# Loading the second weight blocks of summed products through ScalarE's DMA queue instead of SyncE's

## The chip, the cores and the metric

The kernel runs on one core of a Trainium2 chip. The metric is the device time of one execution in microseconds (us); lower is better.

## The reference

Two layers of a residual network, each a full 2048 x 2048 linear layer with bias and a low-rank adapter of rank 16 that is chosen by batch element:

```python
x = x + (x @ W0.T + b0 + (x @ A0[ids0].T) @ B0[ids0].T)
x = x + (x @ W1.T + b1 + 2 * (x @ A1[ids1]) @ B1[ids1])
```

x has 8 batch elements of 512 tokens and 2048 features, all in fp32; ids0 and ids1 name one of 32 adapters for each batch element.

## The kernel before

Since nothing nonlinear stands between the layers, the kernel first makes one matrix of both (V in `v_t`, then the combined matrix in `wc_t`), and then multiplies x by it. A preamble of some 178 us turns layer 0's weights with TensorE and prepares the adapters. Then comes one main loop of six passes. Passes 0 and 1 (`pl < PRE`) multiply the two layers' matrices and read their left operand from `v_t`; passes 2 to 5 multiply the combined matrix `wc_t` with two batch elements each.

Each pass is a 2 x 2 block product by Strassen's scheme: seven products, in the order M5, M3, M2, M4, M1, M7, M6, each of 1024 x 1024 by 1024 x 1024. A product has 16 steps, and a step s is half of a row of tiles: 4 weight tiles of 128 x 128, each multiplied three times against 512 columns (high part times high part, low times high, high times low, L1248 to L1250), which keeps fp32 accuracy. So a step is 12 matmuls. Four of the products (M5, M3, M2, M4) have adapter matmuls between their first steps (L1179, L1182, L1183), and in the later passes M3, M4, M7 and M6 have short ones at their ends (L1193).

In five of the seven products (M5, M2, M1, M7, M6) the weight operand is a sum or a difference of two blocks of the matrix. For a step of these, two blocks of 256 KB come from memory: the **first** into one of four buffers `w_raw` (`RAW`), the **second** into one of three buffers `w_second` (`RAW2`). From there:

- GpSimd (POOL) adds the second to the first in place (L710), once both semaphores, `wa_loaded` and `wb_loaded`, say that the blocks have landed, and counts up `w_summed`.
- ScalarE (ACT) rounds the sum to its high part `w_hi` (L752, `w_split_hi`), in a ring of three, so it also waits for the step three before (`step_done`).
- VectorE (DVE) subtracts it from the sum for the low part `w_lo` (L862), and TensorE (PE) starts the step when `w_lo_ready` says so.

In M3 and M4 the weight operand is one block, and POOL has nothing to do.

All transfers are issued by SyncE (SP), in one order written out in the program. In turn g of its loop SP calls `load_w(g + 6)`. That waits until `w_lo` of the step four before is made, issues the first block (L468), waits until the sum of the step three before is made, and issues the second block (L474). Behind that in the same turn stand loads of the x operand for this or the next pass (L480, L483, most of them in M7 and M6 and in M3), adapter blocks (L514), and stores of finished output tiles (L556, L559), each with its own waits. ACT makes the high part of step g + 2 in its turn g, then high parts of x (L765) and of the adapter (L780).

At the end of the preamble SP issues eight x loads, the adapter blocks, and the loads of steps 0 to 3; the second block of step 3 needs the first sum. Only behind it stand two stores of V (L443), sixteen x loads (L480), a store of 2 MB (`ag_t`, L635), which waits for VectorE, and the loads of step 4.

```python
                if s >= RAW:
                    sp.wait_ge(w_lo_ready, s - RAW + 1)
                (oh, dh), *second = PRODUCTS[i][1]
```

Of the kernel before, what the change touches and what calls it, by code (L numbers as in the profile page):

```python
# [4 lines left out]
P = 128  # L5
# [12 lines left out]
PRODUCTS = (  # L18
# [7 lines left out]
)  # L26
NPROD = len(PRODUCTS)
M5, M3, M2, M4, M1, M7, M6 = range(NPROD)
# [18 lines left out]
def two_layer_lora_kernel(nc, x_t, ids0, ids1, w0_t, w1_t, bias0, bias1,  # L47
# [6 lines left out]
    BATCH, KT, _, T = x_t.shape  # L54
    MT = w0_t.shape[0]
    DIM = KT * P
    SLOTS, RANK, _ = lora_b0.shape
    MH = MT // 2
    KH = KT // 2
    KS = KH // 2  # L60
    SW = KS * P
# [3 lines left out]
    STEPS = MH * 2  # L65
    RAW = 4
    RAW2 = 3
# [6 lines left out]
    PRE = MT * P // (2 * T)  # L74
    NPL = PRE + BATCH // 2
    NQ = NPL * NPROD
    NG = NQ * STEPS
# [3 lines left out]
    ORDER = [(2 * mp + mm, h) for mp in range(MH // 2) for h in range(2) for mm in range(2)]  # L81
# [59 lines left out]
    def x_tiles_at(g, at):  # L141

        out = []
        for k in range(KH):
            q, j = divmod(g - at[k], STEPS)
            if j == 0 and 0 <= q < NQ - 1:
                out.append((q + 1, k))
        return sorted(out)
# [9 lines left out]
    def is_sum_w(g):  # L158
        return len(PRODUCTS[(g // STEPS) % NPROD][1]) == 2

    SUM_STEPS = [0]
# [5 lines left out]
    NU = len(UNITS)  # L167
# [14 lines left out]
    with ctx:  # L182
# [236 lines left out]
        def w_source(pl):  # L419
            return v_t if pl < PRE else wc_t  # L420
# [10 lines left out]
        def _(sp):  # L431
# [17 lines left out]
            def load_w(s):  # L449
                q, j = divmod(s, STEPS)  # L450
                pl, i = divmod(q, NPROD)
                m, h = ORDER[j]
                r = s % RAW
                w_t = w_source(pl)
                if s == 0:
                    for i_v in range(2):
                        sp.wait_ge(v_stored[i_v], 8 * 16 // 2)
                if s == M2 * STEPS:
                    for i_v in range(2):
                        sp.wait_ge(v_stored[i_v], NU * 16 // 2)  # L460
                if pl == PRE and j == 0 and i in (M5, M2):
                    for b in range(4):
                        sp.wait_ge(out_stored[b], (PRE if i == M2 else 1) * MH * 16)
                if s >= RAW:
                    sp.wait_ge(w_lo_ready, s - RAW + 1)
                (oh, dh), *second = PRODUCTS[i][1]
                col = (dh * KH + h * KS) * P
                sp.dma_start(w_raw[:, r, :], w_t[oh * MH + m, :, col:col + SW]).then_inc(wa_loaded[r], 16)  # L468
                for oh, dh in second:
                    n = SUM_STEPS[s]  # L470
                    if n >= RAW2:
                        sp.wait_ge(w_summed, n - RAW2 + 1)
                    col = (dh * KH + h * KS) * P
                    sp.dma_start(w_second[:, n % RAW2, :], w_t[oh * MH + m, :, col:col + SW]  # L474
                                 ).then_inc(wb_loaded[n % RAW2], 16)

            def load_x(pl, half, th, k):
                b = block_no(half, th)
# [159 lines left out]
            for g in range(NG):  # L638
                q, j = divmod(g, STEPS)
                pl, i = divmod(q, NPROD)  # L640
                s = g + 6
# [72 lines left out]
        def _(act_e):  # L714
# [29 lines left out]
            def w_split_hi(s):  # L744
                r = s % RAW
                if is_sum_w(s):
                    act_e.wait_ge(w_summed, SUM_STEPS[s + 1])
                else:
                    act_e.wait_ge(wa_loaded[r], (s // RAW + 1) * 16)
                if s >= RING:  # L750
                    act_e.wait_ge(step_done, s - RING + 1)
                nc.scalar.activation(flat(w_hi[:, s % RING, :, :]), w_raw[:, r, :], ACT.Copy).then_inc(w_hi_ready, 1)  # L752
# [30 lines left out]
            def h_split_hi(pl, th):  # L783
# [4 lines left out]
                else:  # L788
# [3 lines left out]
                nc.scalar.activation(h_split[:, th, :], h_acc[:, :], ACT.Identity,  # L792
                                     bias=h_bias[:, b:b + 1]).then_inc(h_hi_ready, 1)


            for n in range(4):
                t_copy(n, flat(b0t_raw[:, 4 * n:4 * n + 4, :]))
# [24 lines left out]
                        t_copy(Q_USE + i, quarter(q_rows, i))  # L822
            for dg in range(GROUPS - 1):
                copy_g(dg)
            w_split_hi(0)
            w_split_hi(1)
            w_split_hi(2)
            act_e.wait_ge(g_done, NU)
            copy_g(GROUPS - 1)
            act_e.wait_ge(v_stored[0], NU // 2 * 16)  # L830
# [8 lines left out]
            for g in range(NG):  # L839
                q, j = divmod(g, STEPS)  # L840
                pl, i = divmod(q, NPROD)
                if 3 <= g + 2 < NG:
                    w_split_hi(g + 2)
                for qq, k in x_tiles_at(g, X_HI_AT):
                    x_split_hi(qq, k)
                if j == 4 and i in (M4, M3) and pl >= PRE:
                    h_split_hi(pl, DOWN[i][0])
                for b in b_units_at(g, B_SPLIT_AT):
                    b_split_hi(*b)
                if (v := a_unit_at(g)) is not None and v >= PRE * 4:  # L850
                    a_split_hi(v)
# [454 lines left out]
```

## Time and profile before

| | us |
|---|---|
| median of 3 runs | 2192.92 (2192.86 to 2193.49) |
| the profiled execution | 2191.75 |
| its span, first to last instruction | 2190.0 |
| mean granted TensorE clock | 0.979 of full speed |

In the rows further down, a start is counted in us from the first instruction. PE is TensorE's matmuls, PEld its weight loads, DVE VectorE, ACT ScalarE, POOL GpSimd; SPq is SyncE's issuing of a DMA, whose span is the issue, not the transfer. The bracket at the end of a timeline row is idle time of that engine ahead of the instruction, with what ended it. A DMA's time to landing is counted from its issue to its semaphore.

### The profile page before, as it was taken

How to read it: one execution, taken by the hardware profiler on the slowest of the kernel's cores; microseconds unless marked ns; L12 is line 12 of the kernel's file. 1: busy time of each engine (PE TensorE's matmuls, PEld its weight loads, DVE VectorE, ACT ScalarE, POOL GpSimd, SP SyncE). 2: the span in 40 equal slices, each digit the busy share in tenths (PEclk: the TensorE clock that was granted, in tenths of full speed). 3: DMA queues.
4: the chain of work that ended last, by engine and by line, in shares of the span. 5: the costliest groups of instructions: out<-in, count | busy, mean ns of one | idle time of the engine just before them, and what ended most of it. 6: DMA issues, size and time to landing. Idle time of an engine off the chain costs nothing.

```text
span 2190.0 us, 27298 instructions
## 1 busy us (share of the span) xinstructions
PE 2085.6 (95%) x9196; PEld 1716.8 (78%) x9196; DVE 1545.9 (71%) x2137; ACT 726.9 (33%) x1264; POOL 685.9 (31%) x490
## 2 busy tenths in 40 slices
PE   4857999999999999999999999999999999999999
PEld 3745878787878788888788888887888887888787
DVE  2316777886677976777875767875776876777875
ACT  4632222332222333333333333333333333333332
POOL 0002130444221445321354321444322344322343
PEclk8978999999999999999999999999999999999999
DMA  8989564789574789574689564689664689564686
GB/s 235 353 235 320 166 204 138 216 243 303 181 221 124 218 225 318 170 215 126 204 239 314 178 210 129 213 234 312 181 196 143 209 238 307 185 199 136 195 222 198
DMA packets 322104, 473.74 MB, mean 216 GB/s; under 512 B 27948, under 2 KB 120108, under 8 KB 321580
## 3 DMA queue, kind: packets, MB, share of 16 engines
q1 hardware_dynamic: 321964, 471.99, 71.4%
q8 instruction: 74, 1.21, 0.2%
q14 instruction: 66, 0.54, 0.1%
HBM read 394.28 MB, written 77.60 MB: 215 GB/s over the span
## 4 chain that ended last, share of the span: by engine, by line
PE 72%; DMA 12%; DVE 6%; SPq 5%; issue 2%; POOL 2%; ACT 1%; DVEq 0%; POOLq 0%; ACTq 0%
PE acc L1248 22%; PE acc L1250 22%; PE acc L1249 21%; DMA w_second<-wc_t 6%; DMA w_second<-v_t 2%; DVE w_lo L862 2%; PE h_acc L1179 2%; PE h_acc L1183 2%; POOL w_raw L710 2%; DMA pb_t<-b1d_rows 1%; SPq L480 1%; DVE c_out L997 1%; DMA v_t<-v_raw 1%; SPq L468 1%; PE acc L1193 1%
## 5 line engine op out<-in xcount | busy, mean ns | idle before, releaser
L710 POOL TENSOR_TENSOR w_raw<-w_raw,w_second 128x512 f32<-128x512 f32 x480 | 684.4, 1427 | 1489.5 <-DMA w_second<-wc_t 855.9
L1248 PE MATMUL acc<-xop_hi,w_hi 128*128 128x512 f32 x2688 | 1054.6, 392 | 22.3 <-DVE w_lo L862 17.6
L1249 PE MATMUL acc<-xop_hi,w_lo 128*128 128x512 f32 x2688 | 1050.4, 391 | 0.0
L1250 PE MATMUL acc<-xop_lo,w_hi 128*128 128x512 f32 x2688 | 1050.3, 391 | 0.0
L862 DVE TENSOR_TENSOR w_lo<-w_raw,w_hi 128x512 fp32r<-128x512 f32 x672 | 582.8, 870 | 437.8 <-ACT w_hi L752 433.1
L752 ACT ACTIVATE w_hi<-w_raw 128x512 fp32r<-128x512 f32 x672 | 423.7, 631 | 1211.1 <-PE acc L1250 995.2
L1248 PEld LDWEIGHTS acc<-xop_hi,w_hi 128*128 128x128 f32 x2688 | 506.8, 189 | 139.5 <-DVE w_lo L862 29.3
L1250 PEld LDWEIGHTS acc<-xop_lo,w_hi 128*128 128x128 f32 x2688 | 506.4, 188 | 105.6
L1249 PEld LDWEIGHTS acc<-xop_hi,w_lo 128*128 128x128 f32 x2688 | 506.8, 189 | 104.0
L874 DVE TENSOR_TENSOR x_sum<-x_in 128x512 f32<-128x512 f32 x240 | 215.4, 909 | 0.0
L997 DVE TENSOR_TENSOR c_out<-acc,c_out 128x512 f32<-128x512 f32 x304 | 202.2, 682 | 7.9 <-PE acc L1193 6.2
L884 DVE TENSOR_TENSOR xop_lo<-x_sum,xop_hi 128x512 fp32r<-128x512 f32 x240 | 156.2, 682 | 0.3
L765 ACT ACTIVATE xop_hi<-x_sum 128x512 fp32r<-128x512 f32 x240 | 135.5, 588 | 35.4 <-DVE x_sum L874 35.2
L857 DVE TENSOR_TENSOR v_lo<-v_raw,v_hi 128x2048 fp32r<-128x2048 f32 x16 | 36.7, 2292 | 82.7 <-ACT v_hi L734 82.7
L884 DVE TENSOR_TENSOR xop_lo<-x_in,xop_hi 128x512 fp32r<-128x512 f32 x96 | 90.8, 980 | 1.4 <-ACT xop_hi L765 1.3
L1179 PE MATMUL h_acc<-xop_hi,a_split 128*128 128x512 f32 x192 | 77.0, 401 | 9.0 <-issue 9.0
L905 DVE SCALAR_TENSOR_TENSOR b_split<-b_raw,b_split 32x128 fp32r<-32x128 f32 x128 | 48.4, 378 | 48.5 <-ACT b_split L780 45.2
L1183 PE MATMUL h_acc<-xop_lo,a_split 128*128 128x512 f32 x192 | 76.7, 399 | 0.0
L780 ACT ACTIVATE b_split<-b_raw 128x128 fp32r<-128x128 f32 x128 | 38.9, 304 | 98.7 <-DMA b_raw<-pb_t 98.3
L994 DVE SCALAR_TENSOR_TENSOR c_out<-acc,c_bias,x_in 128x512 f32<-128x512 f32 x96 | 71.3, 743 | 0.0
L1107 PE MATMUL x_sum<-ident,w_in 128*128 128x128 f32 x192 | 29.9, 303 | 34.8 <-ACT v_raw L718 34.8
L1107 PEld LDWEIGHTS x_sum<-ident,w_in 128*128 128x128 f32 x192 | 25.8, 159 | 38.2 <-issue 36.9
(101 smaller groups left out, 784.7 us busy)
## 6 DMA issues: line engine op xcount, KB each, us to landing
w_raw<-wc_t SPq DMA_DIRECT2D x448, 256.0 KB, 3.8
w_second<-wc_t SPq DMA_DIRECT2D x320, 256.0 KB, 4.9
w_raw<-v_t SPq DMA_DIRECT2D x224, 256.0 KB, 4.0
w_second<-v_t SPq DMA_DIRECT2D x160, 256.0 KB, 4.9
x_in<-x_t SPq DMA_DIRECT2D x128, 256.0 KB, 6.2
out_t<-c_out SPq DMA_DIRECT2D x128, 256.0 KB, 5.3
w_in<-w_t SPq DMA_DIRECT2D x16, 1024.0 KB, 6.8
v_t<-v_raw SPq DMA_DIRECT2D x16, 1024.0 KB, 8.6
```

Of the source, the lines that this page charges most:

```text
L710: nc.gpsimd.tensor_tensor(w_raw[:, r, :], w_raw[:, r, :], w_second[:, n % RAW2, :], ALU.add if sign > 0 else ALU.subtract).then_inc(w_summ ...
L752: nc.scalar.activation(flat(w_hi[:, s % RING, :, :]), w_raw[:, r, :], ACT.Copy).then_inc(w_hi_ready, 1)
L765: nc.scalar.activation(xop_hi[:, n % XRING, :], src, ACT.Copy).then_inc(x_hi_ready, 1)
L862: nc.vector.tensor_tensor(flat(w_lo[:, s % RING, :, :]), w_raw[:, s % RAW, :], f(flat(w_hi[:, s % RING, :, :])), ALU.subtract).then_inc(w_ ...
L874: nc.vector.tensor_tensor(x_sum[(n_sums(q) + k) % XS][:, :], x_tile(q, 0, k), x_tile(q, 1, k), ALU.add if sign > 0 else ALU.subtract).then ...
L884: nc.vector.tensor_tensor(xop_lo[:, n % XRING, :], src, f(xop_hi[:, n % XRING, :]), ALU.subtract).then_inc(x_lo_ready, 1)
L997: nc.vector.tensor_tensor(c, bank[:, :], old, ALU.add).then_inc(c_updated, 1)
L1179: nc.tensor.matmul(h_acc[:, :], cols, xop_hi[:, n % XRING, :], start=(k == 0 and which == 0), stop=False)
L1183: mm = nc.tensor.matmul(h_acc[:, :], cols, xop_lo[:, n % XRING, :], start=False, stop=end)
L1248: nc.tensor.matmul(bank[:, :], wh, xh, start=(k == 0), stop=False)
L1249: nc.tensor.matmul(bank[:, :], wl, xh, start=False, stop=False)
L1250: mm = nc.tensor.matmul(bank[:, :], wh, xl, start=False, stop=end)
```

## The change

The second blocks are no longer issued by SP. A new function `load_second(s)` in ScalarE's program issues them, with the waits that went with them: for V's stores ahead of step 0 and of M2, for the output stores of earlier passes ahead of pass 2's M5 and M2, and for the sum of the step three before. The order is: three second blocks ahead of the first high part, then behind each high part of step s the second block of step s + 3, where that step has one. SP's `load_w` keeps the first blocks and its own wait. The numbers of blocks, buffers and bytes stay as they were.

```diff
--- before.py
+++ after.py
@@ -463,16 +463,9 @@
                         sp.wait_ge(out_stored[b], (PRE if i == M2 else 1) * MH * 16)
                 if s >= RAW:
                     sp.wait_ge(w_lo_ready, s - RAW + 1)
-                (oh, dh), *second = PRODUCTS[i][1]
+                (oh, dh), *_ = PRODUCTS[i][1]
                 col = (dh * KH + h * KS) * P
                 sp.dma_start(w_raw[:, r, :], w_t[oh * MH + m, :, col:col + SW]).then_inc(wa_loaded[r], 16)
-                for oh, dh in second:
-                    n = SUM_STEPS[s]
-                    if n >= RAW2:
-                        sp.wait_ge(w_summed, n - RAW2 + 1)
-                    col = (dh * KH + h * KS) * P
-                    sp.dma_start(w_second[:, n % RAW2, :], w_t[oh * MH + m, :, col:col + SW]
-                                 ).then_inc(wb_loaded[n % RAW2], 16)
 
             def load_x(pl, half, th, k):
                 b = block_no(half, th)
@@ -792,6 +785,30 @@
                 nc.scalar.activation(h_split[:, th, :], h_acc[:, :], ACT.Identity,
                                      bias=h_bias[:, b:b + 1]).then_inc(h_hi_ready, 1)
 
+            def load_second(s):
+
+                if s >= NG or not is_sum_w(s):
+                    return
+                q, j = divmod(s, STEPS)
+                pl, i = divmod(q, NPROD)
+                m, h = ORDER[j]
+                oh, dh = PRODUCTS[i][1][1]
+                n = SUM_STEPS[s]
+                if s == M5 * STEPS:
+                    for i_v in range(2):
+                        act_e.wait_ge(v_stored[i_v], 8 * 16 // 2)
+                if s == M2 * STEPS:
+                    for i_v in range(2):
+                        act_e.wait_ge(v_stored[i_v], NU * 16 // 2)
+                if pl == PRE and j == 0 and i in (M5, M2):
+                    for b in range(4):
+                        act_e.wait_ge(out_stored[b], (PRE if i == M2 else 1) * MH * 16)
+                if n >= RAW2:
+                    act_e.wait_ge(w_summed, n - RAW2 + 1)
+                col = (dh * KH + h * KS) * P
+                act_e.dma_start(w_second[:, n % RAW2, :], w_source(pl)[oh * MH + m, :, col:col + SW]
+                                ).then_inc(wb_loaded[n % RAW2], 16)
+
 
             for n in range(4):
                 t_copy(n, flat(b0t_raw[:, 4 * n:4 * n + 4, :]))
@@ -822,9 +839,11 @@
                         t_copy(Q_USE + i, quarter(q_rows, i))
             for dg in range(GROUPS - 1):
                 copy_g(dg)
-            w_split_hi(0)
-            w_split_hi(1)
-            w_split_hi(2)
+            for s in range(3):
+                load_second(s)
+            for s in range(3):
+                w_split_hi(s)
+                load_second(s + RAW2)
             act_e.wait_ge(g_done, NU)
             copy_g(GROUPS - 1)
             act_e.wait_ge(v_stored[0], NU // 2 * 16)
@@ -841,6 +860,7 @@
                 pl, i = divmod(q, NPROD)
                 if 3 <= g + 2 < NG:
                     w_split_hi(g + 2)
+                    load_second(g + 2 + RAW2)
                 for qq, k in x_tiles_at(g, X_HI_AT):
                     x_split_hi(qq, k)
                 if j == 4 and i in (M4, M3) and pl >= PRE:
```

The first place is the start of the main loop, on ACT. Before, ACT there copies quarters of `g_rows` from PSUM, makes three high parts, and copies the last quarter:

```order
L742 ACTIVATE g_rows<-acc 128x512 [waits g_done,t_filled]
L742 ACTIVATE g_rows<-acc 128x512 [waits g_done] x2
L752 ACTIVATE w_hi<-w_raw 128x512 [waits w_summed] x3
L742 ACTIVATE g_rows<-acc 128x512 [waits g_done]
L718 ACTIVATE ag<-x_sum 128x8x4x16 [waits t_filled,v_lo_ready,v_stored0]
```

Now (the lines of the new file stand 7 lower where they are below the diff's first part; L809 is the issue in `load_second`):

```order
L735 ACTIVATE g_rows<-acc 128x512 [waits g_done,t_filled]
L735 ACTIVATE g_rows<-acc 128x512 [waits g_done] x2
L809 DMA w_second<-v_t 128x512 [waits v_stored1,v_stored0]
L809 DMA w_second<-v_t 128x512 x2
L745 ACTIVATE w_hi<-w_raw 128x512 [waits w_summed]
L809 DMA w_second<-v_t 128x512 [waits w_summed]
L745 ACTIVATE w_hi<-w_raw 128x512 [waits w_summed]
L809 DMA w_second<-v_t 128x512 [waits w_summed]
L745 ACTIVATE w_hi<-w_raw 128x512 [waits w_summed]
L809 DMA w_second<-v_t 128x512 [waits w_summed]
L735 ACTIVATE g_rows<-acc 128x512 [waits g_done]
```

Six issues of second blocks now stand on ACT between the third and the last copy to `g_rows`. Three of them are ahead of the first high part.

The second place is SP in M6 of pass 2, where the next pass's x is loaded (L483), with adapter blocks (L514) and output stores (L559) between. Before:

```order
L468 DMA w_raw<-wc_t 128x512 [waits w_lo_ready]
L474 DMA w_second<-wc_t 128x512 [waits w_summed]
L483 DMA x_in<-x_t 128x512
L514 DMA b_raw<-pb_t 128x1x128 [waits b_lo_ready]
L559 DMA out_t<-c_out 128x512 [waits c_updated]
L468 DMA w_raw<-wc_t 128x512 [waits w_lo_ready]
L474 DMA w_second<-wc_t 128x512 [waits w_summed]
L483 DMA x_in<-x_t 128x512
L514 DMA b_raw<-pb_t 128x1x128 [waits b_lo_ready]
L559 DMA out_t<-c_out 128x512 [waits c_updated]
L468 DMA w_raw<-wc_t 128x512 [waits w_lo_ready]
L474 DMA w_second<-wc_t 128x512 [waits w_summed]
```

Now, for the same stretch (L476 is the x load, L507 the adapter block, L552 the output store):

```order
L468 DMA w_raw<-wc_t 128x512 [waits w_lo_ready]
L476 DMA x_in<-x_t 128x512
L507 DMA b_raw<-pb_t 128x1x128 [waits b_lo_ready]
L552 DMA out_t<-c_out 128x512 [waits c_updated]
L468 DMA w_raw<-wc_t 128x512 [waits w_lo_ready]
L476 DMA x_in<-x_t 128x512
L507 DMA b_raw<-pb_t 128x1x128 [waits b_lo_ready]
L552 DMA out_t<-c_out 128x512 [waits c_updated]
L468 DMA w_raw<-wc_t 128x512 [waits w_lo_ready]
```

A turn of SP loses one issue of four or five, and with it the wait for `w_summed`; the others keep their order and their waits.

## Rows read from the trace of the kernel before

**Rows 1.** The page: busy us by engine; the group of w_lo; landings of second blocks.

```profile
PE 2085.6 (95%) x9196; PEld 1716.8 (78%) x9196; DVE 1545.9 (71%) x2137; ACT 726.9 (33%) x1264; POOL 685.9 (31%) x490
...
L862 DVE TENSOR_TENSOR w_lo<-w_raw,w_hi 128x512 fp32r<-128x512 f32 x672 | 582.8, 870 | 437.8 <-ACT w_hi L752 433.1
...
w_second<-wc_t SPq DMA_DIRECT2D x320, 256.0 KB, 4.9
```

**Rows 2.** Waits of PE from 200 us on: total us, times, longest.

```profile
PE acc L1248 <- DVE w_lo L862: 17.6, 14, 6.2
```

**Rows 3.** Timeline of PE: the first step, and four of its fourteen waits for a low part.

```profile
177.66 0.76 PE L1248 MATMUL acc<-xop_hi,w_hi 128*128 128x512 f32 x1 [4.40 <-DVE xop_lo L884]
...
202.59 0.79 PE L1248 MATMUL acc<-xop_hi,w_hi 128*128 128x512 f32 x1 [6.21 <-DVE w_lo L862]
...
740.64 0.50 PE L1248 MATMUL acc<-xop_hi,w_hi 128*128 128x512 f32 x1 [1.84 <-DVE w_lo L862]
...
1531.47 0.50 PE L1248 MATMUL acc<-xop_hi,w_hi 128*128 128x512 f32 x1 [0.81 <-DVE w_lo L862]
...
1860.72 0.50 PE L1248 MATMUL acc<-xop_hi,w_hi 128*128 128x512 f32 x1 [0.76 <-DVE w_lo L862]
```

**Rows 4.** Chain of waits around 1190 us: start us, us, what.

```profile
1177.53 0.65 SPq L468
...
1178.22 8.34 DMA w_second<-wc_t
...
1186.69 1.30 POOL w_raw L710
...
1188.01 0.64 ACT w_hi L752
...
1188.68 1.81 DVE w_lo L862
```

**Rows 5.** Issues of first blocks (L468), second blocks (L474), 1145 to 1210 us.

```profile
L468 SPq DMA_DIRECT2D w_raw<-wc_t x21: 319/320/1364, 1146.1 to 1209.9; - x21
...
DMA to landing us min/median/max: 3.0/6.8/8.7
...
L474 SPq DMA_DIRECT2D w_second<-wc_t x20: 319/437/912, 1147.2 to 1207.4; - x20
...
DMA to landing us min/median/max: 3.3/6.8/8.5
```

**Rows 6.** Stretches: us, busy of PE, PEld, DVE, ACT, POOL, clock, DMA share, GB/s.

```profile
202.00:205.00 3.00, 2.41 (x6) 1.94 (x7) 3.00 (x6) 1.26 (x2) 2.27 (x2) 0.50 0.91 255
...
240.00:290.00 50.00, 50.00 (x222) 41.43 (x221) 38.61 (x58) 14.92 (x25) 7.37 (x5) 1.00 0.58 168
1145.00:1210.00 65.00, 64.04 (x282) 52.17 (x280) 40.88 (x58) 22.48 (x45) 31.42 (x22) 1.00 0.95 303
```

**Rows 7.** Waits of SP's queue: the one for a sum.

```profile
SPq L474 <- POOL w_raw L710: 81.7, 87, 5.3
```

**Rows 8.** Timeline of SP at the end of the preamble.

```profile
168.42 0.32 SPq L474 DMA_DIRECT2D w_second<-v_t  x1
...
189.06 2.02 SPq L468 DMA_DIRECT2D w_raw<-v_t  x1
191.13 1.18 SPq L474 DMA_DIRECT2D w_second<-v_t  x1
```

**Rows 9.** Timeline of ACT there, and POOL's sum for step 4.

```profile
163.57 1.55 ACT L742 ACTIVATE g_rows<-acc 128x512 f32<-128x512 f32 x3
168.43 0.63 ACT L752 ACTIVATE w_hi<-w_raw 128x512 fp32r<-128x512 f32 x1 [3.31 <-POOL w_raw L710]
...
171.98 0.58 ACT L742 ACTIVATE g_rows<-acc 128x512 f32<-128x512 f32 x1
...
199.37 4.30 POOL L710 TENSOR_TENSOR w_raw<-w_raw,w_second 128x512 f32<-128x512 f32 x3 [26.29 <-DMA w_second<-v_t]
```

**Rows 10.** Timeline of PE behind its wait at 202.59 us.

```profile
206.15 0.40 PE L1250 MATMUL acc<-xop_lo,w_hi 128*128 128x512 f32 x1
```

## The prediction

> **What bounds the kernel now.** I read the page first, then PE's waits, then the chain of waits and the timelines at the places those name. TensorE is busy for 2085.6 us, 95% of the span, ScalarE for 33% [rows 1]. In an undisturbed stretch PE takes 222 matmuls in 50 us, so 0.225 us each [rows 6], and a step of 12 takes 2.7 us. A change to the weight loads can only give back time in which PE waited for weights. From 200 us on that is 17.6 us in 14 waits [rows 2]. They have three causes, told apart by what ends the chain of waits ahead of each:
>
> - One wait of 6.21 us at step 4, ended at 202.59 [rows 3]. The chain ahead of it is the second block of step 4, issued at 191.13 [rows 8], POOL's sum at 199.37 [rows 9], then the high and low parts.
> - Eight waits of 0.25 to 0.81 us, 4.68 us in all, between 525 and 1861 us; the longest, at 1531.47, and the last stand in [rows 3]. All lie where M6 gives way to the next pass's M5. There the chain goes through second blocks: one issued at 1178.22, landed 8.34 us later, then sum 1.30, high part, low part 1.81 [rows 4].
> - Five waits, 6.77 us in all, such as the 1.84 us at 740.64 [rows 3]. Ahead of them VectorE is busy without a gap. Weights are not what it lacks, and I leave them as they are.
>
> **The change, part by part.**
>
> *SP sheds 480 issues and the waits for sums.* Those waits are 81.7 us, 87 of them [rows 7]; an issue takes 0.32 us at least and 0.44 in the middle of the dense stretch [rows 5]. SP is not on PE's path where its loads are early, so most of this is worth nothing: in the stretch from 240 to 290 us transfers run at 168 GB/s and PE has no gap [rows 6]. It counts where SP is late, in M6.
>
> *ACT takes 480 issues.* By 0.44 us that is 211 us, on top of 727 busy, so 43% of the span. An issue stands behind a high part and ahead of x's high parts, so it delays those by 0.44 us, by up to 2.02 us where the queues are full (the longest issue in [rows 8]). A high part is made in turn g for step g + 2, two steps or 5.4 us ahead; it and the low part take 0.63 [rows 9] and 0.87 [rows 1], which leaves 3.9 us. I cost ACT's issues at nothing: the cover is this lead. Without it each would cost its 0.44.
>
> *When a second block is issued.* Before: behind the low part of step s - 4 and the sum of step s - 3. Now: behind the high part of step s - 3, which itself waits for that sum and for the step six before to end. With all on time that is one to two us later than before, in a chain of 0.63 (high part) + 0.44 (issue) + 4.9 (the landing in the middle of all, [rows 1]) + 1.3 (sum, [rows 4]) = 7.3 us against the three steps, 8.1 us, until the high part of step s is due. So it hides. In M6 the old second issue already waited for that sum, so nothing is lost there by the later place, only 0.1 to 0.6 us for the high part ahead.
>
> *The dense stretch (M6 to M5).* Transfers run at 303 GB/s with a share of 0.95, and both blocks take 6.8 us in the middle, up to 8.5 and 8.7 [rows 5, 6]. A loop of landing 6.8, sum 1.3, and wake-ups of 0.2 for three buffers gives 2.8 us a step, and with 8.34 it gives 3.3: above the 2.7 of PE. That loop is what the eight waits are. Now a second block no longer queues behind x, adapter and output transfers of its own queue. How fast it lands from a queue of its own no row shows. The bounds are the fastest landing of the stretch, 3.3 us, and the slowest, 8.5. At 5 the loop, with 0.63 for the high part ahead of the issue, is (5 + 1.3 + 0.2 + 0.63)/3 = 2.4 us and no longer binds; at 8.5 it is 3.5. I take about 5, near the 4.9 of [rows 1], since a step's second block is only 262 KB of the 820 KB that 303 GB/s move in a step. The first blocks stay behind x and stores. They are issued 0.7 us ahead of the second now (1177.53 against 1178.22 [rows 4]), and SP no longer stops for sums ahead of them, so by themselves they land 0.7 us and more earlier than the second did: enough for a wait of 0.25 to 0.81. Against that, they share the bandwidth with a queue that is always served. I count 70% of the 4.68, **-3.3 us**.
>
> The Trainium skill (DMA: Bandwidth & Descriptors, Queues, rings and completion order) says each DMA engine takes packets round-robin from the queue rows that have work; by that rule the seconds get up to half the bandwidth and all 4.68 us of their waiting could go, unless the firsts turn late.
>
> *The start.* Before, SP stood at step 3's second block until 168.42 [rows 8] for the first sum, by the program 5.3 us, the longest of its kind [rows 7]. Two stores of V and sixteen x loads stood behind it. Now they go out some 5 us earlier. In exchange, the seconds of steps 0 to 2 are issued on ACT behind three copies, at 163.57 + 1.55 = 165.1 [rows 9], into full queues. If the first lands 3.3 us later, the fastest of [rows 5], its sum ends at 169.7 and the high part that began at 168.43 [rows 9] comes 1.3 us late; with 8 us it comes 6 us late. The last copy to `g_rows`, at 171.98 [rows 9], and PE's first step, at 177.66 [rows 3], move by about as much. But PE then had 6.21 us to wait at step 4. Step 4 is set by volume: x loads, 2 MB of `ag_t`, then its blocks, into queues so full that one issue took 2.02 us [rows 8]. Step 4's second block is now out long before, behind the second high part, and one block of 262 KB more (step 5's, 0.8 us) is ahead of its first. So the delay of the first step runs into the wait at step 4, and step 4 starts where it did, within 1.5 us. What I count is the clock. Behind the wait the granted clock is 0.50 (1.2 GHz) [rows 6] after PE stood for 6.21 us; the 8 matmul starts from 202.59 to 206.15 [rows 3, 10] take 3.56 us where 8 x 0.225 = 1.8 would do. With a wait of 2 us or less I expect, as behind the 1.84 us at 740.64, a smaller loss: **-1.6 us**. The bounds are +3 (the first step 6 us late and `ag_t`'s turn late with it) and -7.9 (wait and clock loss both gone).
>
> *The sum.* -3.3 - 1.6 = -4.9 us against the profiled execution's 2191.75, that is 2186.9. The median of the runs is 1.17 us above that execution, so I predict 2192.92 - 4.9 = **2188.0 us**.
>
> **The rivals.** A measurement of this kernel can tell about 0.2%, 4.4 us, from no change.
>
> *A. It is volume, not order.* In M6 the two weight blocks, x, stores and adapter blocks need 32 + 16 + 8 blocks of 262 KB and 8 of 66 KB, 15.2 MB in 16 steps; at 303 GB/s that takes 50 us where PE needs 16 x 2.7 and 8 short matmuls, 45. If the engines are the limit, a sum waits for whichever block lands last, and moving one to another queue only swaps which. At the start the same holds. For it: a share of 0.95 in the stretch [rows 6]. Against it: SP's waits for sums leave gaps in its issue, and the chain names second blocks. Time: 2192 us, between 2189 and 2195. Chance 0.30.
>
> The Trainium skill (DMA: Bandwidth & Descriptors, Issuing engines are not separate DMA queues) says that DMAs started by several engines run on the same 16 DMA engines and interleave, and only the sequencer's issue time is saved; that is this rival, and no row of the kernel before can test it.
>
> *B. The first blocks turn late.* The one that ends slower. The SP queue keeps 6.8 us x 303 GB/s = 2.06 MB in flight; if the seconds take their 262 KB in each 2.7 us, 96 GB/s, off the top, the same 2.06 MB take 2.06 MB / 207 GB/s = 9.95 us. A first block's loop has four buffers: (9.95 + 1.3 sum + 0.63 high + 0.87 low)/4 = 3.2 us a step, 0.5 above PE's 2.7. Over M6's 16 steps that is 8 us, less the lead of 3.9, so 4 us in each of five changes of pass: +20 us gross, in place of the 4.68, so +15, 2207 us. It decides where the landing of first blocks passes 4 x 2.7 - 2.8 = 8.0 us. Against it: no more bytes are asked for, so by the time a first block lands only up to two more seconds than before can have passed it, 1.7 us; that gives 8.5 us and some +2 to +6 rather than +15. Chance 0.14, mostly in the lower part, 2195 to 2204.
>
> *C. The start is worse and the clock too.* ACT waits for sums ahead of the last `g_rows` copy, PE starts 6 us late, and `ag_t` behind VectorE goes out after a gap in the transfers; or POOL's sums now fall on VectorE's busy parts. With nothing gained in M6: +3 to +8, 2196 to 2201. Chance 0.10.
>
> The change does what it says: 480 issues leave SP and appear on ACT in the same order of blocks, so that rival is void.
>
> **How the numbers follow.** My forecast has 0.46, A 0.30, B 0.14, C 0.10. Forecast means faster by over 0.2% (2188.5 or less), A means within, B and C slower by over 0.2%. The low end is all of it gained: 4.68 + 7.9 = 12.6, 2180.3, so 2181. The high end takes in C and the lower part of B: 2202.
>
> **What would show it.** Right: SP's waits for sums gone; ACT's DMA issues with 0.32 to 0.5 us in the middle; second blocks that land in 5 us or so from 1145 to 1210, first blocks under 8; no PE wait above 0.3 us between M6 and M5; PE's first step 1 to 5 us later, its wait at step 4 under 3 us, and granted clock above 0.8 behind it. Wrong: first blocks over 8 us with PE waits of several us in each M6 (B); landings of both unchanged near 6.8 (A); step 4 later than 205 us (C). The five waits under a busy VectorE should stay within 1 us of what they were.

## The result, and the profile after

Against the seven runs of the kernel before it, the changed kernel took 2182.43 us (median of 7 runs, 2179.93 to 2187.83; before 2193.49). The ratio is 0.9937, 95% interval 0.9918 to 0.9956. Three more comparisons of the same two kernels gave 0.9976 (0.9958 to 0.9995), 0.9956 (0.9937 to 0.9974) and 0.9964 (0.9945 to 0.9982). All four intervals lie below 1. The mean over the 43 runs of the change in them is 2185.7 us and over the 86 runs of the kernel before 2194.9, a gain of **9.2 us, 0.4%**. The standard deviation of single runs is over 4 us, and the first comparison, 12.9 us between its means, was a lucky one. The forecast was 4.9 us.

The profiled execution took 2179.93 us. Its page: span and busy time, a part of the DMA queues (q10 is ScalarE's), the chain's engines, the group of w_lo, and the issues:

```profile
span 2178.2 us, 27304 instructions
PE 2078.1 (95%) x9196; PEld 1712.3 (79%) x9196; DVE 1538.4 (71%) x2137; ACT 726.3 (33%) x1264; POOL 675.6 (31%) x490
...
q1 hardware_dynamic: 252844, 346.13, 51.8%
q10 hardware_dynamic: 69120, 125.86, 18.9%
...
PE 80%; DVE 7%; DMA 6%; issue 3%; SPq 2%; ACT 1%; POOL 0%; ACTq 0%; DVEq 0%; POOLq 0%
...
L882 DVE TENSOR_TENSOR w_lo<-w_raw,w_hi 128x512 fp32r<-128x512 f32 x672 | 572.7, 855 | 437.8 <-ACT w_hi L745 433.7
...
w_second<-wc_t ACTq DMA_DIRECT2D x320, 256.0 KB, 4.3
```

126 MB go through a queue of their own now. The second blocks land in 4.3 us in the middle, 4.9 before [rows 1]. PE is busy 7.5 us less for the same 9196 matmuls (2085.6 us before [rows 1]), so most of the gain stands in PE's busy time and not in its waits. That repeats: 2077.0 to 2079.3 in the change's three other profiles, 2085.8 in a second one of the kernel before. VectorE's 1538.4 for 1545.9 us does not repeat: that second profile has 1539.8, and the change's others 1520.0 to 1542.5.

PE's waits for a low part, in total, in number and the longest, have hardly changed:

```profile
PE acc L1268 <- DVE w_lo L882: 16.2, 14, 6.3
```

That is 1.4 us less than in [rows 2]. Nor does this view hold the rest of the span's 11.8 us, since it leaves out the preamble, the lower clock behind a wait and the scatter of each. The profiles need a ruler that takes in everything. ScalarE makes one high part for each of the 672 steps, in order, at PE's pace. I take the time from the one of step 4 to the one of step 116 as pass 0. (A high part can be made several us ahead of its step, 7.4 at step 116 before and 9.8 now, so where one part of a pass ends and the next begins is good to some 2 us.) Here are these two starts, of the kernel before and of the change, from ScalarE's timelines:

```profile
200.66 0.63 ACT L752 ACTIVATE w_hi<-w_raw 128x512 fp32r<-128x512 f32 x1 [17.16 <-POOL w_raw L710]
...
538.76 0.63 ACT L752 ACTIVATE w_hi<-w_raw 128x512 fp32r<-128x512 f32 x1 [2.86 <-POOL w_raw L710]
```

```profile
196.10 0.63 ACT L745 ACTIVATE w_hi<-w_raw 128x512 fp32r<-128x512 f32 x1 [17.36 <-POOL w_raw L703]
...
526.52 0.63 ACT L745 ACTIVATE w_hi<-w_raw 128x512 fp32r<-128x512 f32 x1 [1.07 <-POOL w_raw L703]
```

Pass 0 took 338.1 us before and 330.4 now. By the same ruler the first profiles differ by +1.7 us in pass 1 and by -1.3 in passes 2 to 5. What lay ahead of step 4 differs by 4.6 us, and most of that is older than the change. The high part of V's fourteenth unit, ahead of every new instruction, began at these times before and after:

```profile
150.14 1.91 ACT L734 ACTIVATE v_hi<-v_raw 128x2048 fp32r<-128x2048 f32 x1
```

```profile
145.99 1.91 ACT L727 ACTIVATE v_hi<-v_raw 128x2048 fp32r<-128x2048 f32 x1
```

So 4.15 of the 11.8 us between the two profiles is not the change's. The next run bears this out: the changed kernel's second profile has this row at 150.34.

### The profile page after: what moved, and what is told of

Its sections match the earlier page's. It is cut to its first block, busy times and chain, and to the rows that moved or that the text cites. A ratio compares the mean times of both kernels' runs of the same rounds, so it can differ in the third digit from the quotient of the medians.

```text
span 2178.2 us, 27304 instructions
## 1 busy us (share of the span) xinstructions
PE 2078.1 (95%) x9196; PEld 1712.3 (79%) x9196; DVE 1538.4 (71%) x2137; ACT 726.3 (33%) x1264; POOL 675.6 (31%) x490
## 4 chain that ended last, share of the span: by engine, by line
PE 80%; DVE 7%; DMA 6%; issue 3%; SPq 2%; ACT 1%; POOL 0%; ACTq 0%; DVEq 0%; POOLq 0%
PE acc L1268 24%; PE acc L1269 24%; PE acc L1270 24%; PE h_acc L1199 2%; PE h_acc L1203 2%; DVE w_lo L882 2%; DMA b_raw<-pb_t 2%; DVE xop_lo L904 1%; DMA pb_t<-b1d_rows 1%; PE acc L1213 1%; DMA v_t<-v_raw 1%; DVE c_out L1017 1%; DVE x_sum L894 1%; DMA w_second<-v_t 1%; DMA w_raw<-v_t 1%
## 5 line engine op out<-in xcount | busy, mean ns | idle before, releaser
L703 POOL TENSOR_TENSOR w_raw<-w_raw,w_second 128x512 f32<-128x512 f32 x480 | 674.0, 1406 | 1488.2 <-DMA w_second<-wc_t 469.6
L882 DVE TENSOR_TENSOR w_lo<-w_raw,w_hi 128x512 fp32r<-128x512 f32 x672 | 572.7, 855 | 437.8 <-ACT w_hi L745 433.7
L904 DVE TENSOR_TENSOR xop_lo<-x_in,xop_hi 128x512 fp32r<-128x512 f32 x96 | 94.2, 1013 | 1.3 <-ACT xop_hi L758 1.1
L925 DVE SCALAR_TENSOR_TENSOR b_split<-b_raw,b_split 32x128 fp32r<-32x128 f32 x128 | 48.5, 379 | 50.7 <-ACT b_split L773 47.6
```

The costliest lines, as they stand in the source:

```text
L703: nc.gpsimd.tensor_tensor(w_raw[:, r, :], w_raw[:, r, :], w_second[:, n % RAW2, :], ALU.add if sign > 0 else ALU.subtract).then_inc(w_summ ...
L882: nc.vector.tensor_tensor(flat(w_lo[:, s % RING, :, :]), w_raw[:, s % RAW, :], f(flat(w_hi[:, s % RING, :, :])), ALU.subtract).then_inc(w_ ...
L904: nc.vector.tensor_tensor(xop_lo[:, n % XRING, :], src, f(xop_hi[:, n % XRING, :]), ALU.subtract).then_inc(x_lo_ready, 1)
```

## The experiments

Each was timed against the kernel before on the same chip. Lengths by the ruler stand in a table behind them.

**The change again.** No edit.

> The changed kernel once more, to tell what repeats. Theory N (noise in the preamble): 4.2 of the 11.8 us between the two profiled executions lay ahead of the first new instruction (the high part of unit 13 of V began at 145.99 us in place of 150.14), and that part is chance; then the ratio to the kernel before comes nearer 0.996 than 0.9937, and that high part begins anywhere from 145 to 151 us. Theory S (systematic): ratio 0.993 to 0.995 again and the start near 146.

Measured: ratio 0.9976 (0.9958 to 0.9995), and the preamble's row at 150.34 us. Theory N, chance in the preamble, was right. The size came out smaller still, and the two intervals do not meet, so comparisons differ by more than the interval within one of them shows.

**ScalarE's queue in pass 0 only, and in passes 1 to 5 only.**

```diff
-                for oh, dh in second:
+                for oh, dh in (() if on_act(s) else second):
...
-                if s >= NG or not is_sum_w(s):
+                if s >= NG or not is_sum_w(s) or not on_act(s):
```

with `on_act(s)` being `s < NPROD * STEPS` in the one and `s >= NPROD * STEPS` in the other.

> ScalarE's queue loads second blocks in pass 0 only, SP's in passes 1 to 5 as before. In the profiles nearly all of the gain behind the preamble lay in pass 0 (7.6 us between step 4 and pass 1's M5), and passes 1 to 5 gave nothing in sum. If that is systematic: 5 to 8 us faster than before, as fast as the whole change. If it was chance in which sums of POOL fell on VectorE's instructions, the gain is in proportion to the passes, 1 to 3 us.

> The complement: ScalarE's queue loads second blocks in passes 1 to 5 only. If the gain is pass 0's: within 2 us of the kernel before. If the gain is the dense stretches from M6 to M5 (my prediction: 3.3 us there): 2 to 4 us faster.

Measured: 0.9976 (0.9961 to 0.9992) and 0.9975 (0.9959 to 0.9991), beside 0.9976 of the whole on that chip. Means against the kernel before: -5.2, -5.6 and -6.4 us. Each half is worth something of its own, so neither place has all the gain. That the halves add up to the whole is not shown; with intervals of 3.5 us either side it is not denied.

**SP alone, the second block one step late.**

```diff
                 sp.dma_start(w_raw[:, r, :], w_t[oh * MH + m, :, col:col + SW]).then_inc(wa_loaded[r], 16)
-                for oh, dh in second:
-                    ...
+                if s >= 1:
+                    load_second(s - 1)
+                if s == NG - 1:
+                    load_second(s)
```

> No second queue: SP issues all blocks, but each second block one step later in its program, behind the first block of the next step, where its wait for a sum is always met. If the gain comes from SP no longer standing at that wait, or from the later moment of the sums against VectorE's work, this has most of it: 5 us or more faster. If it comes from the second queue (its own place at the DMA engines, SP's shed issues), this is within 3 us of the kernel before, or slower, since the second blocks now queue behind x and stores for one step more.

Measured: 1.025 (1.022 to 1.0279), 53 us slower by the means. SP's wait for a sum hardly ever holds it here (6.0 us in all, against 81.7 [rows 7]), and that did not help. PE's waits for low parts:

```profile
PE acc L1259 <- DVE w_lo L873: 53.3, 49, 10.7
```

**The change, the second block one high part later.**

```diff
-                    load_second(g + 2 + RAW2)
+                    load_second(g + 1 + RAW2)
```

> As the change, but each second block is issued on ScalarE's queue one high part later. On SP's queue one step of delay cost 54 us. If a queue of its own gives the second blocks their slack (they pass the x loads and stores), this costs 0 to 15 us against the change. If the moment of issue alone counts, whichever queue it is, it costs about the same 50 us.

Measured: 1.0108 (1.0077 to 1.0139), 25 us slower than before by the means and 35 us slower than the change, which was timed on the same chip (below). PE's waits:

```profile
PE acc L1269 <- DVE w_lo L883: 47.4, 48, 5.5
```

Neither theory's number came (0 to 15 us or about 50); the truth lies between. An estimate from the program, with the durations of a high and a low part: the issue lies, counted from the start of the step five before, at about -0.9 us in the kernel before (behind a low part), 0 in the change, +1.8 in the SP kernel above and +2.7 in this one. The latest of the four costs half of what the second latest costs. So on a queue of their own the blocks have more room. But the moment still counts: one step later takes away the whole gain and more.

**The kernel before, again.**

> The kernel before, profiled once more, to have two profiles of it on each question. If pass 0's loss is systematic, it takes 338 us again between the high parts of step 4 and of step 116 (338.1 in the first profile, 338.7 in the kernel that leaves pass 0 to SP), against 330 to 334 us where ScalarE's queue loads pass 0. If it is chance, anything between. Ratio to itself: 1 within its interval.

Measured: 0.9996 (0.9973 to 1.0018). Pass 0 took 339.8 us. The profiled execution took 2203.43 us, against a median of 2195.28. Its passes 2 to 5 took 1312.1 us where the first profile had 1302.3, and PE waited longer:

```profile
PE acc L1248 <- DVE w_lo L862: 26.9, 21, 6.9
```

The 4.68 us that I counted out of one profile came from an execution shorter than most.

**The change, a third time.**

> The changed kernel once more beside it, since the first comparison gave a ratio of 0.9937 and the second 0.9976. If both are draws of one effect of some 9 us with several us of scatter between chips and executions: 0.995 to 0.997, pass 0 in 330 to 334 us, and from the first high part to the fifth 30.5 to 30.9 us in place of 32.1.

Measured: 0.9956 (0.9937 to 0.9974); pass 0 in 333.0 us, both as expected. The first to the fifth high part took 31.6 us, longer than expected.

**POOL's sums later in pass 0, all loads on SP.**

```diff
                     pool.wait_ge(wb_loaded[n % RAW2], (n // RAW2 + 1) * 16)
+                    if 2 <= s < NPROD * STEPS:
+                        pool.wait_ge(w_lo_ready, s - 1)
```

> The kernel before with one more wait, in pass 0: POOL adds the blocks of step s only once the low part of step s - 2 is made, about when the change lets it. All loads stay with SP. If pass 0's gain came from where POOL's sums fall against VectorE's work, pass 0 takes 330 to 335 us here too, and the kernel is 3 to 6 us faster than before. If it came from the blocks' landing or from SP, pass 0 stays at 338 us or gets slower, since sums can now only be later.

Measured: 0.9988 (0.997 to 1.0006), so not told from no change, with a mean 2.5 us lower. But pass 0 took 332.6 us against 338 to 340, by a wait that can only hold POOL back. Where it comes from is in a table of pass 0:

| pass 0, us | M5 | M3, M2 | M4, M1 | M7, M6 |
|---|---|---|---|---|
| before, two profiles | 42.3, 42.5 | 105.2, 105.1 | 97.5, 99.7 | 93.0, 92.5 |
| change, four profiles | 41.9 to 43.8 | 103.3 to 106.3 | 94.2 to 94.8 | 89.6 to 90.8 |
| SP, sums later | 43.0 | 103.7 | 93.6 | 92.3 |

In M4 and M1 the later sums alone give all that the change gives. In M7 and M6 they give next to nothing, and the change gives 2 to 3 us. This says too much for the change, because high parts run ahead of PE there: from PE's own first matmuls, M7 and M6 take 89.3 and 89.4 us before, 88.0 to 88.4 in the change and 88.6 with the later sums. By the same starts of PE, pass 0, from step 4 to the first step of pass 1, takes 326.7 and 328.6 us before, 320.6 to 324.3 in the change's four profiles and 320.8 with the later sums alone, and nearly all of it is one product, M1:

| M1 of pass 0, us | before, two profiles | change, four profiles | SP, sums later |
|---|---|---|---|
| first matmul of M1 to first of M7 | 48.5, 50.7 | 45.2 to 45.8 | 44.6 |
| its 17 VectorE instructions from the low part of its first step through that of its third | 12.0, 12.8 | 10.9 to 11.5 | 10.2 |
| mean granted clock of TensorE | 0.96, 0.93 | 1.00 | 1.00 |

The profiles of the other kernels agree. Where SP loads pass 0 and the sums have no wait of their own, M1 takes 48.4 us (ScalarE in passes 1 to 5 only) and 50.1 (half second blocks, further down). Where ScalarE's queue loads the second blocks of pass 0, it takes 44.6 to 45.9 us in four more. With both blocks on ScalarE's queue (further down) it takes 48.1, and 47.4 and 47.8 in the two kernels that issue a step late: a second queue alone does not shorten M1, the moment of the sums does.

The mechanism is in the durations. VectorE has no gap around the low parts of M1's second and third step, for which PE waits. Before, from the timelines of POOL, VectorE and PE:

```profile
390.24 1.82 POOL L710 TENSOR_TENSOR w_raw<-w_raw,w_second 128x512 f32<-128x512 f32 x1 [1.68 <-DMA w_second<-v_t]
...
390.84 1.78 DVE L946 SCALAR_TENSOR_TENSOR c_acc<-x_in,bias,c_acc 128x512 f32<-128x512 f32 x1
...
393.74 1.56 DVE L862 TENSOR_TENSOR w_lo<-w_raw,w_hi 128x512 fp32r<-128x512 f32 x1
...
400.22 0.50 PE L1248 MATMUL acc<-xop_hi,w_hi 128*128 128x512 f32 x1 [1.81 <-DVE w_lo L862]
```

After:

```profile
382.48 0.75 DVE L966 SCALAR_TENSOR_TENSOR c_acc<-x_in,bias,c_acc 128x512 f32<-128x512 f32 x1
...
384.27 1.29 POOL L703 TENSOR_TENSOR w_raw<-w_raw,w_second 128x512 f32<-128x512 f32 x1 [2.35 <-DMA w_second<-v_t]
...
384.34 1.77 DVE L882 TENSOR_TENSOR w_lo<-w_raw,w_hi 128x512 fp32r<-128x512 f32 x1
...
391.32 0.50 PE L1268 MATMUL acc<-xop_hi,w_hi 128*128 128x512 f32 x1 [1.14 <-DVE w_lo L882]
```

The same addition to `c_acc` takes 1.78 us beside a sum and 0.75 without one. Now it falls between two sums. PE's waits in M1 went from 2.80 to 1.43 us, and behind them the clock fell no more: the granted clock (column PEclk, the third from the right) of the whole of M1, before and after:

```profile
391.50:440.00 48.50, 45.70 (x193) 37.03 (x192) 42.80 (x55) 14.21 (x25) 23.40 (x17) 0.96 0.70 208
```

```profile
384.60:430.10 45.50, 44.07 (x193) 35.87 (x192) 38.49 (x53) 14.18 (x24) 22.90 (x17) 1.00 0.71 214
```

The Trainium skill (SBUF — State Buffer, Who interferes with whom) says a VectorE instruction with two SBUF inputs and a GpSimd instruction that reads SBUF lock each other out, the second to issue waiting for the first; these rows agree in kind, 1.03 us longer beside a sum of 1.82.

In M2 PE waits behind VectorE too, at an adapter matmul (4.54 us before). There the change's first profile had 3.66 us, but its others have 4.53, 4.28 and 4.28: that gain was chance.

**The change with that wait in M2 and M1 of pass 0.** Twice.

```diff
+                    if s < NPROD * STEPS and s // STEPS in (M2, M1):
+                        pool.wait_ge(w_lo_ready, s - 1)
```

> The change, and POOL's wait for the low part of step s - 2 in M2 and M1 of pass 0, where that wait alone took 8 us off two products with all loads on SP. If the change's gain in pass 0 is the same thing (POOL's sums off VectorE's busy parts), little is left: within 2 us of the change. If the two add, pass 0 takes 326 to 329 us and the kernel is 3 to 5 us faster than the change, near 0.994 of the kernel before.

> The change with POOL's later sums in M2 and M1 of pass 0, once more. Its first profile had pass 0 in 331.7 us against 330.4, 333.0 and 333.0 of the change, so the profile speaks for no more than 1 us of gain, though its ratio (0.9932) was the best so far. If the profile is right: within 2 us of the change on this chip. If the ratio is: 4 us or more faster than it.

Measured: 0.9932 (0.9909 to 0.9955), and then 0.9971 (0.9952 to 0.999) where the change itself had 0.9964 (0.9945 to 0.9982) on the same chip. The profile was right: no gain on top that can be told. The profiles show why little was left: with this wait M1 of pass 0 takes 44.6 us by PE's starts, where the change alone takes 45.2 to 45.8.

The expectation for the change on that chip, whose ratio stands above:

> The changed kernel, on one chip with the next two, so that they can be set against it. Ratio to before near the mean of the three comparisons so far (0.9937, 0.9976, 0.9956): 0.994 to 0.998.

**Both blocks on ScalarE's queue.**

```diff
             def load_w(s):
+                if s >= RAW:
+                    return
...
+                if s >= RAW:
+                    act_e.wait_ge(w_lo_ready, s - RAW + 1)
+                    oh, dh = PRODUCTS[i][1][0]
+                    col = (dh * KH + h * KS) * P
+                    act_e.dma_start(w_raw[:, s % RAW, :], w_source(pl)[oh * MH + m, :, col:col + SW]
+                                    ).then_inc(wa_loaded[s % RAW], 16)
```

> Both blocks of every step from step 4 on go through ScalarE's queue, behind the high part of step s - 3; SP keeps x, adapter blocks and stores. If what matters is that weights needn't queue behind x and stores, this gains in the stretches from M6 to M5: 3 to 10 us faster than the change. If the two queues share the engines by halves, the weights (524 KB a step, 193 GB/s) get less than they need beside a queue of x and stores, and each first block is also issued later: 10 to 60 us slower than before.

Measured: 0.9972 (0.995 to 0.9994), 5.6 us faster than before by the means and not told apart from the change. Neither theory's number came. Second blocks landed in 5.0 us in the middle here, as slowly as on SP:

```profile
w_second<-wc_t ACTq DMA_DIRECT2D x320, 256.0 KB, 5.0
```

From 1145 to 1210 us it was 6.5 us, with first blocks at 5.6. So what lets them land sooner in the change is having no first block ahead of them, more than having no x there. At the start, the weights of step 4 now passed the x loads, and the fifth high part came 17.6 us behind the first instead of 32.2; but M5 then took 54.3 us instead of 42.3, and the sum of the two is 71.9 against 74.5, and 72.6 to 75.5 in the change's four profiles. The wait only moved from the weights to x. That fits a start bound by its bytes, which no run here tests by itself.

**Half of each second block, on SP and with the change.** Both kernels leave out the other half of each second block, so their results are not the product. They only price the bytes.

```diff
+                    c = SW if n < RAW2 else SW // 2
-                    sp.dma_start(w_second[:, n % RAW2, :], w_t[oh * MH + m, :, col:col + SW]
+                    sp.dma_start(w_second[:, n % RAW2, 0:c], w_t[oh * MH + m, :, col:col + c]
```

> The kernel before with only the first 256 of 512 columns of each second block loaded (the sum's other half uses old data), so 63 MB fewer bytes on the same queue in the same order. If the stretches from M7 to M5 are bound by the bytes (rival A), they lose their excess over an undisturbed pass: some 10 to 15 us in all. If order and waits bind them, they stay near the 700 us of the kernel before.

> The change with half of each second block left out (the other half of the sum uses old data). With all loads on SP halving them took some 10 us, 13 us of it in the stretches from M7 to M5 of passes 1 to 4 (551.6 us against 556.9 to 566.9). If the change's gain in those stretches is room for the bytes' queueing, the same thing, the two don't add: these stretches take 550 to 554 us again, 0 to 5 us less than the change's 553.0 to 558.7. If order and bytes are two separate losses: under 546 us.

Measured: 0.9946 (0.9926 to 0.9965) and 0.9925 (0.9907 to 0.9943), by the means 11.5 and 17.9 us faster than before, where the change on the second one's chip had 8.5. By the ruler, the last column from the fifth high part of M7 to that of the next pass's M3:

| us | pass 0 | passes 2 to 5 | M7 to M5, passes 1 to 4 |
|---|---|---|---|
| before, first and second profile | 338.1, 339.8 | 1302.3, 1312.1 | 556.9, 566.9 |
| ScalarE in pass 0 only | 333.7 | 1313.8 | 568.2 |
| SP, sums later in pass 0 | 332.6 | 1311.4 | 566.6 |
| the change, four profiles | 330.4, 333.0, 333.0, 334.7 | 1301.0, 1300.5, 1302.3, 1297.7 | 554.1, 553.0, 558.7, 554.6 |
| ScalarE in passes 1 to 5 only | 338.7 | 1305.2 | 559.4 |
| the change, sums later in M2 and M1 of pass 0, two profiles | 331.7, 330.5 | 1304.7, 1300.6 | 562.8, 557.8 |
| half second blocks, SP | 334.5 | 1295.1 | 551.6 |
| half second blocks, the change | 328.5 | 1299.8 | 550.6 |

The last column holds the dense stretches. Four profiles with SP loading them average 564.7 us, seven with the second queue 557.2 (the change's own four 555.1), and both kernels with half the blocks 551.1. So queueing behind bytes costs some 13 to 14 us there and the second queue takes back some 7, more than half. Two of the four SP profiles took longer than is usual for their kernels (2203.43 us where the median is 2195.28, 2201.42 where it is 2188.68), so 7 is rather too much; the runs with ScalarE in passes 1 to 5 only say 5.6 us. Halving the blocks on top of the second queue gives these stretches nothing beyond what halving them alone gives: here it is one loss. Over the whole kernel the two nearly add, because the second queue's gain in M1 of pass 0 is another (50.1 us there with half blocks on SP, 44.9 with the change).

## Why the prediction was wrong, and where it was right

**The size came out twice the forecast.** Forecast -4.9 us; the first comparison gave 11 between the medians, and all four together 9.2. The range (2181 to 2202) held the median of 2182.43, near its end. Two terms carry the error.

*The dense stretches, -3.3 us.* The mechanism was the one described, second blocks that land late behind their queue; that the three buffers make the loop was argued, and no run changed their number. The term was mis-sized, because it was summed over the waits of one execution, [rows 2, 3], and taken at 70%. The kernel before waits for low parts for 17.6 us in one profile and 26.9 in the next, and its dense stretches take 556.9 or 566.9. The gain there is 5.6 us by the runs and some 7 by the profiles, for 3.3. PE's waits from M7 to M5 add up to 4.7 and 10.3 us before and 3.4 to 5.6 in the change's four profiles. So they did not go away, and "no PE wait above 0.3 us between M6 and M5" did not come: the first profile still has four of 0.74 to 1.09 us, the longest this one:

```profile
1200.01 0.50 PE L1268 MATMUL acc<-xop_hi,w_hi 128*128 128x512 f32 x1 [1.09 <-DVE w_lo L882]
```

I had "about 5" for the landing; it is 5.8 in the middle (5.5 to 5.9 in the four profiles) against 6.8 [rows 5], from 1145 to 1210 us, second blocks and then first blocks:

```profile
L809 ACTq DMA_DIRECT2D w_second<-wc_t x20: 326/326/327, 1146.9 to 1207.7; - x20
...
DMA to landing us min/median/max: 2.9/5.8/8.5
```

```profile
L468 SPq DMA_DIRECT2D w_raw<-wc_t x22: 319/320/1408, 1145.4 to 1209.4; - x22
...
DMA to landing us min/median/max: 3.0/6.3/10.1
```

*The waits under a busy VectorE, 0 us.* "I leave them as they are" was the step that failed outright. The chain of waits named VectorE there, and I stopped at the name. VectorE was busy partly because POOL's sums held it up, and the change moves those sums. All five waits lie in M1, of passes 0, 1, 2 and 5. In pass 0 M1 gets 3 to 5 us shorter, by shorter waits and by a clock that no longer falls behind them, and later sums with all loads on SP do this by themselves. In the other passes nothing of the kind can be told: the first profile of the change has 7.6 us of such waits in M1 over all passes for 6.8 before, since pass 1's grew. So "within 1 us of what they were" came true of the total, by luck, and hid that pass 0's had been halved. I had this as a mishap of rival C ("POOL's sums now fall on VectorE's busy parts") and not as a gain, although nothing spoke for one sign rather than the other.

*The start, -1.6 us.* The mechanism was wrong, and the size came out near it by luck. PE still waited at step 4, at full length, and the clock fell behind it as before:

```profile
172.82 0.76 PE L1268 MATMUL acc<-xop_hi,w_hi 128*128 128x512 f32 x1 [2.72 <-DVE xop_lo L904]
...
197.89 0.80 PE L1268 MATMUL acc<-xop_hi,w_hi 128*128 128x512 f32 x1 [6.25 <-DVE w_lo L882]
```

```profile
196.00:202.00 6.00, 4.11 (x11) 3.27 (x12) 5.24 (x9) 2.49 (x4) 4.72 (x4) 0.54 0.91 292
```

Counted from the fourteenth unit of V, PE's first step came 0.7 us earlier and not 1 to 5 later (26.83 against 27.52), and step 4 came 0.5 us earlier (51.90 against 52.45). Over all profiles step 4 came at 51.2 to 51.9 in the change against 52.5 and 53.2 before, so about 1 us was gained here. That step 4 stays about where it was held. That the earlier step would be late did not: the seconds were not issued "behind three copies". The rows of ScalarE and its queue show why:

```profile
157.56 1.92 ACT L727 ACTIVATE v_hi<-v_raw 128x2048 fp32r<-128x2048 f32 x1
157.77 1.31 ACTq L809 DMA_DIRECT2D w_second<-v_t  x3
159.38 1.55 ACT L735 ACTIVATE g_rows<-acc 128x512 f32<-128x512 f32 x3
```

*ACT's issues, 0 us.* Right, and cheaper than thought: 0.326 us in the middle and 0.453 at most, never the 2.02 I feared, and most of them overlap the activation in front of them. ScalarE stayed at 33%.

*Rival A* (volume, no change) is refuted as a whole, since all four comparisons lie under 1. But its argument fits the start, and in the dense stretches bytes are indeed the root: halving the second blocks frees 13 to 14 us, about twice what the second queue frees. The sentence of the Trainium skill (DMA: Bandwidth & Descriptors, Issuing engines are not separate DMA queues) on saving only issue time is not borne out here: at the same bytes the second blocks land sooner, counted from their issue, so it is not issue time alone that was saved. How much of the 9 us is issue time saved on SP was not tried by itself. *Rival B* had the right sign for first blocks in its worst case only: one took 10.1 us where the longest was 8.7 [rows 5]. In the middle they took 6.3 us, and 6.7 to 7.4 in the change's other profiles, about the 6.8 of before and never over 8. *Rival C* did not come: PE's first step was not late. POOL now waits for first blocks too, where before it waited for second blocks alone:

```profile
POOL w_raw L703 <- DMA w_second<-wc_t: 469.6, 189, 50.8
POOL w_raw L703 <- DMA w_second<-v_t: 451.3, 89, 161.6
POOL w_raw L703 <- DMA w_raw<-wc_t: 392.9, 106, 50.1
POOL w_raw L703 <- DMA w_raw<-v_t: 173.6, 58, 51.8
```

**What stays open.** Profiles of the kernel before average 15 us more than the change's, its unprofiled runs 9; two profiles of it are too few to say how much of the difference is chance. So the gains of single parts, read from profiles, add up to more than the kernel gained. Why passes 2 to 5 of one kernel differ by 10 us from one execution to the next was not tried.

## What to carry to other kernels

Read a stall that one profile shows for a kernel near its limit as one draw: a second profile of the same kernel moved the waits of one term of this sum from under 5 us to about 10. When a change shifts when one engine runs, price the engines that slow down beside it, with both signs: compare the duration of the same instruction with and without the other engine's, which takes two rows. And look at the granted clock behind a wait: in M1 of pass 0 it was about half of the gain. A load that is last to land and first to be needed may be worth a queue of its own even where the bytes are the limit, but its moment of issue must not slip: one step later cost 35 us on the second queue and 53 on the first, far more than the queue gained.

## What the runs showed of the hardware

A DMA in ScalarE's program does not wait for the activations ahead of it that it has no semaphore wait on. Three issues stand behind three copies in the program and went out at 157.77 us, 1.6 us before the first copy began, while the activation before was still running; of the 477 later ones 441 begin within 0.03 us of the start of the high part that they follow. An addition or subtraction of two SBUF operands took VectorE 0.69 to 0.75 us alone and 1.77 to 1.78 beside a GpSimd sum. One issue of a 256 KB load took up to 2.02 us on SP's queue in the first profile of the kernel before and up to 4.24 in that of the change (an x load at 165.2 us), and never over 0.453 on the second queue beside it, which carries one block a step. With both blocks of each step on it, that queue's issues of second blocks took up to 1.70 us. In M1 of pass 0 the granted clock fell behind PE waits of 2.8 and 3.7 us in all and stayed at 1.00 in the change's four profiles, where they were 1.1 to 1.7.
